# Two cross attentions and the self attention projections: runtime loops over batch pairs replaced by code written out for all eight batches

## The reference

```python
# layer 0: self attention (16 heads of 16), cross attention (16 heads of 8), gated MLP
x = rms_norm(hidden, ln_in_w)
mixed = where(vm, x @ v_qkv, x @ l_qkv)          # self attention projections
q, k, v = split(mixed); q, k = rotary(q, k)
h = h + where(vm, sdpa(q, k, v) @ v_dense, ... @ l_dense)
ck, cv = split(ctx @ ckv_w)
h = h + sdpa(rms_norm(h) @ cq_w, ck, cv) @ cdense_w    # cross attention 0, 1601 keys
h = h + where(vm, v_mlp(mi), l_mlp(mi))
# layer 1: cross attention (16 heads of 64), key mask, MLP
k, v = split(ctx @ Wkv)
x = x + tanh(attn_gate) * softmax(mask(q @ k.T)) @ v @ Wo   # cross attention 1
x = x + tanh(ff_gate) * gelu(layernorm(x) @ W1) @ W2
# layers 2 and 3: attention over ctx with 256 features, a gate, rms_norm
```

## Time and profile before

| | |
|---|---|
| median of 3 runs | 3548.72 us (3547.68 to 3569.73) |
| the profiled execution: its own time | 3548.34 us |
| its span, from the first instruction to the last | 3546.5 us |
| instructions | 74028 |
| TensorE matmul busy | 3285.9 us, 93% of the span |
| VectorE, ScalarE, GpSimd busy | 55%, 52%, 44% |
| mean granted TensorE clock | 0.972 |
| batches 0 to 5 of cross attention 0, by its marks | 476.15 to 1076.39 us |
| batches 0 to 5 of cross attention 1, by its marks | 1664.39 to 2673.92 us |

### The profile page before, as it was taken

The page is one execution under the profiler, slowest core; times in us unless marked ns, Lnnn a source line. Parts: engine busy times, 40 slices in busy tenths (PEclk is TensorE's granted clock), DMA queues, the critical chain, the costliest instruction groups (busy, mean ns, idle before and its releaser), DMA issues. The chain is left out here.

```text
span 3546.5 us, 74028 instructions
## 1 busy us (share of the span) xinstructions
PE 3285.9 (93%) x25176; PEld 2373.6 (67%) x25176; DVE 1968.1 (55%) x3261; ACT 1833.2 (52%) x3374; POOL 1571.9 (44%) x1421
## 2 busy tenths in 40 slices
PE   7798799898999889998999999999999998999997
PEld 5655644444444378876777777777777776878886
DVE  4465577777777545545655556555555552114544
ACT  2254267676777623335656566556565663323342
POOL 3213022221122111114887788877887884014554
PEclk9899899999999999999999999999999999999998
DMA  4785300000000032221000101010001003210200
GB/s 121 176 125 111 101 7 16 19 16 19 16 18 26 18 131 112 102 93 52 17 32 14 33 14 35 14 33 14 32 29 46 13 15 130 85 67 1 100 7 12
DMA packets 74753, 179.38 MB, mean 51 GB/s; under 512 B 14721, under 2 KB 44929, under 8 KB 68481
## 3 DMA queue, kind: packets, MB, share of 16 engines
q1 hardware_dynamic: 70240, 161.81, 15.3%
q0 software_dynamic: 4128, 12.60, 1.4%
HBM read 115.09 MB, written 59.26 MB: 49 GB/s over the span
## 5 line engine op out<-in xcount | busy, mean ns | idle before, releaser
L1812 DVE TENSOR_REDUCE cross_partmax<-cross_r 128x1 f32<-128x400 f32 (+1 forms) x1024 | 541.9, 570 | 433.2 <-PE cross_r L1897 416.8
L1656 POOL TENSOR_TENSOR cross_acc<-cross_acc,cross_probs 128x512 f32<-128x512 f32 x448 | 573.8, 1281 | 70.0 <-ACT cross_probs L1721 33.4
L1256 DVE TENSOR_REDUCE cross_partmax<-cross_m 128x2 f32<-128x800 f32 (+1 forms) x512 | 497.1, 991 | 182.4 <-PE cross_m L1359 181.4
L1721 ACT ACTIVATE cross_probs<-cross_s,cross_bias 128x512 f32<-128x512 f32 x576 | 354.3, 686 | 355.0 <-PE cross_s L1927 339.0
L1167 ACT ACTIVATE cross_probs<-cross_s 128x512 f32<-128x512 f32 (+1 forms) x832 | 453.2, 595 | 148.4 <-PE cross_s L1379 147.9
L1656 POOL TENSOR_TENSOR cross_acc<-cross_acc,cross_w 128x512 f32<-128x512 f32 (+1 forms) x256 | 327.6, 1280 | 25.4 <-ACT cross_w L1721 1.0
L1106 POOL TENSOR_TENSOR cross_diag<-c_ident,cross_negmax 128x256 fp32r<-128x256 f32 x128 | 75.8, 613 | 495.4 <-DVE cross_negmax L1264 495.4
L1921 PE MATMUL cross_s<-cross_q_hi,cross_k_hi 64*128 64x256 f32 (+1 forms) x1664 | 257.5, 300 | 21.6 <-ACT cross_probs L1721 20.6
L1390 PE MATMUL cross_av<-cross_probs,cross_v 128*32 128x256 f32 (+1 forms) x3328 | 267.7, 393 | 10.1 <-ACT cross_probs L1167 8.7
L1940 PE MATMUL cross_av<-cross_probs,cross_v 128*64 128x256 f32 x2304 | 276.7, 385 | 0.0
L1359 PE MATMUL cross_m<-cross_ks,cross_qd 64*128 64x400 f32 (+1 forms) x1024 | 210.0, 415 | 43.5 <-DVE cross_partmax L1256 35.3
(11 more groups left out here) (304 smaller groups left out, 6891.6 us busy)
## 6 DMA issues: line engine op xcount, KB each, us to landing
d_masked_ctx<-tail_ctx_split SPq DMA_DIRECT2D x8, 1602.0 KB, 5.3
d_self_qk<-selfproj_qk_split POOLq DMA_DIRECT2D x32, 256.0 KB, 5.5
self_qs<-d_self_qk SPq DMA_DIRECT2D x64, 128.0 KB, 8.7
self_ks<-d_self_qk SPq DMA_DIRECT2D x64, 128.0 KB, 9.3
d_cross<-tail_pr SPq DMA_DIRECT2D x8, 1024.0 KB, 4.6
cross_qp<-d_cross SPq DMA_DIRECT2D x64, 128.0 KB, 2.3
d_cross<-cross_out SPq DMA_DIRECT2D x64, 128.0 KB, 1.8
tail_attn<-d_cross SPq DMA_DIRECT2D x8, 1024.0 KB, 5.4
```

The costliest lines, as they stand in the source:

```text
L1256: nc.vector.tensor_reduce(partmax[:, :, jt // 2, jt % 2, i:i + 1], m_pair(sets[q], w), AX.X, ALU.max).then_inc(maxed, 1)
L1656: nc.gpsimd.tensor_tensor(acc[0:w, g % 2], left, prob(t)[0:w], ALU.add).then_inc(added, 1)
L1721: nc.scalar.activation(prob(t)[0:w], src_, ACT.Exp, scale=XHD ** -0.5, bias=bias[0:w, p, t:t + 1]).then_inc(probs_ready, 1)
L1812: nc.vector.tensor_reduce(partmax[:, m, i:i + 1], r_ps[banks[q]][:, 0:KCH[i][1]], AX.X, ALU.max).then_inc(maxed, 1)
```

## The change

The three runtime loops go. `batches` and `units` become Python loops over the eight batches, and so does SyncE's loop in the self attention projections. The order of the work on each engine stays as it was, and so do all buffers, shapes and semaphore counts; every count and address becomes a constant.

```diff
 def batches(eng, ahead, main):
     ahead(0, 0)
-    with eng.Fori(0, B // 2 - 1) as i:
-        ahead(i * 2 + 1, 1)
-        main(i * 2, 0)
-        ahead(i * 2 + 2, 0)
-        main(i * 2 + 1, 1)
-    ahead(B - 1, 1)
-    main(B - 2, 0)
-    main(B - 1, 1)
+    for b in range(B):
+        if b + 1 < B:
+            ahead(b + 1, (b + 1) % 2)
+        main(b, b % 2)
...
-                with sp.Fori(0, B // 2 - 1) as i:
-                    for p in range(2):
-                        sp.wait_ge(x_free, i * 2 + p + 3)
-                        sp.dma_start(x[:, p], src["x_t"][i * 2 + p + 2]).then_inc(x_ready[p], 16)
+                for b in range(2, B):
+                    sp.wait_ge(x_free, b + 1)
+                    sp.dma_start(x[:, b % 2], src["x_t"][b]).then_inc(x_ready[b % 2], 16)
...
-    with eng.Fori(0, B // 2 - 1) as i:
-        batch(i * 2, 0)
-        batch(i * 2 + 1, 1)
-    batch(B - 2, 0)
-    batch(B - 1, 1, last=True)
+    for b in range(B):
+        batch(b, b % 2, last=b == B - 1)
```

## The result

The changed kernel takes 3514.75 us (median of 4 runs, 3512.6 to 3519.49) beside 3548.2 us for the kernel before: a ratio of 0.9894, 95% interval 0.9869 to 0.9919. Two more comparisons, on other occasions, gave 0.9883 (0.9861 to 0.9905) and 0.9897 (0.9875 to 0.9918). The two medians of the first comparison differ by 33.4 us, a ratio of 0.9906, inside its interval. The forecast was 38.8 us less, 3509.9 us, a ratio of 0.9891. It was right in size and sign, and the time lies within the range of 3502 to 3529 us; what follows asks whether it was right for its reasons, since several of its terms were not.

The account below looks back on a forecast made before the run. TensorE, busy for 93% of the span, was taken as the bound, with only idle or late-issue time to win. Gains of 17.0 + 21.2 + 0.6 = 38.8 us took 3548.7 to 3509.9 us; range 3502 to 3529.

Parts of the forecast that it names:

- The back edges: TensorE's four taken loop branches in the cross attentions: 3.5 us each in 0, 6.0 in 1, 19.0 us in all.
- The register arithmetic: Register instructions ahead of waits in loop code: 1.7 us a batch in cross attention 0; 19.8 us without the edges.
- the term of cross attention 1: Six loop batches there replaced by straight ones of 164.54 or 164.89 us: gain 20.2 to 22.3, taken as 21.2 us.
- The units after the stall: Cross attention 1's units 50 to 58, behind step 49's wait for VectorE's query copy: straight batch read as 164.54 us.
- The upper end of the gain: Cross attention 1: gain over six batches if a straight batch takes 164.54 us, 22.3 us.
- nearly all: Cross attention 0: the 1.7 us a batch between loop and straight code called nearly all TensorE idle time between instructions.
- Cross attention 0: Six loop batches of 600.24 us in all replaced by straight ones of 97.20 us each: gain 17.0 us.
- The projections: Self attention projections: gain 0, bounds -1 and +1 us, from batch periods of 14.44 us looped and 14.45 taken as straight.
- Neither shows, so what hides both is the chain of dependent steps: Self attention projections: back edge and register arithmetic said to be hidden by dependent steps from engine to engine; gain 0.
- Ahead of the first marks: About one loop unit ahead of each cross attention's first mark: 0.4 and 0.2 us, together 0.6 us gained.
- The layout rival: New code layout makes fetches late: one gives 3514 to 3516 us, three 3520 to 3528; an earlier start 3506; 20%.
- the slower case: Sequential fetch doesn't keep up, each TensorE block of straight code late; at 0.78 us a block 3586 us; 3%.

Follow-up runs that it names:

- hint kernel: Kernel before with a back-edge prefetch hint on the loops of the batches, register arithmetic kept; ratio 0.9981 (0.9960 to 1.0002).
- regs_kept: Against the kernel before: no back edges, projections straight, register arithmetic kept in batches 0 to 3 of both cross attentions, constants after; 3520.8 us, one execution.

## Why the prediction was right, and where it wasn't

**The back edges (19.0 us).** Right. The long branches are gone from the trace, as is every issue gap of about 3 us inside the cross attentions. The hint kernel took them away alone in cross attention 0, for 7.4 us in six batches, where 2 x 3.5 were forecast. `regs_kept`, which keeps the arithmetic and has no edge, gives 7.7 us there and 11.9 in cross attention 1, where 2 x 6.0 were forecast.

**The register arithmetic (19.8 us).** Right in kind, shown by `regs_kept`; the term of cross attention 1 was too small. A straight batch there is 164.1 to 164.2 us, not 164.54 or 164.89. The units after the stall, from which I read it, held one slow place: in the changed kernel the period from unit 51 to 52 is 19.97 us, and in the kernel before it was 20.30. The upper end of the gain was put at 22.3 us and it was 24.6. One reading beside this term was too strong: of the 1.7 us between a loop batch and a straight one in the earlier trace rows, 0.5 are busy time of TensorE and 1.2 idle, so two thirds is idle time and not "nearly all".

**Cross attention 0 (17.0 us).** Right for the smooth rate (the changed kernel's second profile, with no fall of the clock in these six batches, won 17.3), too large for most executions. The smooth rate is 97.1 to 97.2 us as forecast, but in the straight code the clock fell on its own for 3.4 or 6.8 us at ends of units. Windows of the changed kernel ahead of, in and behind such a fall:

```profile
560.00:566.50 6.50, 5.36 (x44) 2.11 (x42) 5.14 (x6) 3.83 (x8) 1.78 (x3) 1.00 0.01 2
566.60:573.40 6.80, 6.80 (x30) 3.30 (x32) 2.60 (x4) 3.46 (x6) 6.57 (x8) 0.50 0.11 24
573.40:583.55 10.15, 9.98 (x88) 4.19 (x88) 8.33 (x11) 7.89 (x15) 1.34 (x3) 1.00 0.00 0
```

Ahead of it TensorE was busy for 5.36 of 6.5 us, with a wait of 0.85 us for VectorE's maxima as it has at each unit's end; then it is at 0.50 while it is busy all the time. The unit took 26.25 us instead of 23.3. In the eight profiles whose cross attention 0 is straight throughout there are 21 units with such a fall among 256, at 0.7 to 3.0 us each; among the 88 units with register arithmetic (four profiles) there is none apart from the back edges, and among the 40 straight units of those four there is one. Six batches took 582.9 to 590.3 us in those eight, 586.8 on average, so the straight code gave back some 3.6 us of its gain through the clock. The counts say that it goes with the arithmetic's absence; why is open.

**The start of cross attention 1 (0 forecast, +12.3 in the first profile).** Not shown to be the change's: two profiles of the kernel before have 60.6 and 72.3 us. One execution's 60.6 had been read as the stage's length. The same holds for the output layer of self attention. The changed kernel's profiles have 77.3, 79.9 and 79.7 us and those of the kernel before 82.0 and 82.1, which looks like a gain; but two of the versions with throwaway matmuls, whose code is the changed kernel's up to there, have 82.1 and 82.4. The clock was at its lower level for 17 us of it in these two and in the first profile of before, for 6 in the first profile of the changed kernel. Self attention's 172.5 us isn't the change's either: the other straight versions have 174.1 to 174.6, the kernel before 173.6.

**The projections (0 forecast, 0.9 us by the marks, inside the bound of 1).** The step "Neither shows, so what hides both is the chain of dependent steps" was wrong. A batch is 0.15 us shorter on average in straight code. The period that I took as straight, from batch 5 to 6, begins inside the loop's last round and is 14.21 us once the loop is gone, so it still held some of the loop's cost.

**Ahead of the first marks (0.6 us).** Not resolved. From the first matmul of cross attention 0 to its first mark it took 63.1 to 63.7 us in three profiles with loops and 61.9 to 63.3 in the eight straight ones.

**The layout rival (20%).** No late fetch was seen in any straight version; the gaps of TensorE at the starts of phases stayed (7.05 us for 7.10 ahead of cross attention 0, 9.65 for 9.66 ahead of cross attention 1, and the other gaps of over 5 us between phases within 0.4). TensorE's instruction blocks fell from 223 to 203, and the slower case, blocks that come late, has nothing for it.

So the total was right for its two main causes. That it came so close is in part luck. In the first profile the misses on both sides (-3.4 in cross attention 1's rate, -1.9 in the projections, -4.7 in the output layer, +3.9 in cross attention 0, mostly clock, +12.3 of clock at one start, and some of 1 to 2 us elsewhere) happen to offset each other to 3 us. Over many executions what is the change's own offsets too: cross attention 1's rate gave 3.4 us more than forecast and the projections 0.9, and the clock took 3.6 back in cross attention 0. The ratios of 0.9883 to 0.9897 hold the forecast's 0.9891.

## What to carry to other kernels

Where a kernel has its last rounds written out behind a runtime loop, the trace already holds the experiment: compare a batch out of the loop with one out of straight code, by marks, and multiply; it gave a forecast of 38.8 us here where the branch's and the arithmetic's own durations can't be added up. Take that straight batch at a place with no stall ahead of it, and don't take a period that begins in the loop. And before a stage's length out of one profile is used as a fixed number, look at the granted clock in it: the start of cross attention 1, which waits for data, was 12 us longer in the next execution of the same code.

## What the runs showed of the hardware

In the cross attentions a branch back cost TensorE 3.5 to 4.7 us in its sequencer and, in the kernel before, the other four engines at most 0.07 us. It isn't so in every loop: in the short one of the projections TensorE's two branches back took 0.22 and 0.24 us.

```profile
L64 PEldq COMPARE_BRANCH  x3: 83/220/243, 53.9 to 111.3; - x3
```

With the prefetch hint the long ones fell to 0.50 and 0.36 us in one loop and only to 2.96 and 3.37 in the other. The granted clock stayed at its lower level (1.2 GHz) for 48 us at the start of cross attention 1 in the changed kernel's first profile; TensorE stood still for the first 5.7 of them and was busy for 40.0 of the other 42.1. In an execution of the kernel before it was 10 us there and, later on, another 7. From the tail's last matmul to the first mark it took anything from 70 to 83 us in nine profiles without throwaway matmuls, and in three of them 70. With three such matmuls in the wait it was 69 us twice, with five 70.4 once. That fits with their sparing the unlucky case, but three profiles are too few to show it.
